# ScalarE's attention loop over 32 blocks, rolled and written out

## What is computed

```
q = apply_rope(q); k = apply_rope(k)
q = q * (1.0 / jnp.sqrt(jnp.float32(hd)))
scores = jnp.einsum('bhqd,bhkd->bhqk', q, k)
attn = jax.nn.softmax(scores, axis=-1)
out = jnp.einsum('bhqk,bhkd->bhqd', attn, v)
```

## Time and profile before

| | us |
|---|---|
| median of 3 runs (4465.53 to 4467.92) | 4466.51 |
| the profiled execution | 4463.72 |
| its span, first to last instruction | 4462.0 |
| attention's main part in it, first exponential to last copy | 685.94 to 3382.3 |
| PE busy | 4160.7 (93%) |
| DVE busy | 3137.1 (70%) |
| ACT busy | 2665.3 (60%) |

### The profile page before, as it was taken

How to read it: one execution, slowest core, us unless ns; L and a number is a source line. 1 busy time by engine, 2 the same in 40 slices (tenths; PEclk the granted TensorE clock), 3 DMA queues, 4 the chain that set the end, 5 groups by cost and what they waited for, 6 DMA issues and landing times. The chain is left out here.

```text
span 4462.0 us, 71502 instructions
## 1 busy us (share of the span) xinstructions
PE 4160.7 (93%) x23748; PEld 1788.7 (40%) x23748; DVE 3137.1 (70%) x4158; ACT 2665.3 (60%) x5113; POOL 374.6 (8%) x444
## 2 busy tenths in 40 slices
PE   6988637999999999999999999999998899999999
PEld 4666401222222222222222222222225788876666
DVE  6877596999999999999999999999950011132332
ACT  4555304778777778778778778778784222222122
POOL 0222355000000000000000000000001000011110
PEclk8999758999999999999999999999999999999999
DMA  4232393000004000004000000000004755532221
GB/s 149 76 104 90 113 152 116 6 4 4 6 4 73 12 4 4 6 4 72 14 4 4 6 4 4 6 4 4 6 4 161 230 193 195 198 100 73 64 60 40
DMA packets 206165, 264.69 MB, mean 59 GB/s; under 512 B 24880, under 2 KB 169520, under 8 KB 204240
## 3 DMA queue, kind: packets, MB, share of 16 engines
q1 hardware_dynamic: 193872, 228.98, 17.8%
q0 software_dynamic: 11904, 31.10, 2.4%
HBM read 184.76 MB, written 74.97 MB: 58 GB/s over the span
## 5 line engine op out<-in xcount | busy, mean ns | idle before, releaser
L1172 ACT ACTIVATE a_PT<-a_PS 128x512 f32<-128x512 f32 x4096 | 2119.2, 603 | 687.6 <-PE a_PS L1046 608.3
L1253 DVE TENSOR_REDUCE a_MX<-a_PS 128x2 f32<-128x1024 f32 x1062 | 1290.6, 1221 | 149.0 <-PE a_PS L1031 136.0
L1259 DVE TENSOR_REDUCE a_MX<-a_PS 128x1 f32<-128x512 f32 x1972 | 1266.7, 684 | 66.2 <-PE a_PS L1031 45.6
L1046 PE MATMUL a_PS<-a_QS,a_KS 128*128 128x512 bf16 x4096 | 1075.5, 383 | 24.2 <-ACT a_PT L1172 9.5
L1056 PE MATMUL a_OT<-a_PT,a_VG 128*32 128x512 f32 x8192 | 1095.2, 607 | 0.9 <-ACT a_PT L1172 0.8
L1031 PE MATMUL a_PS<-a_KS,a_QS 64*128 64x512 bf16 x4096 | 731.5, 393 | 111.5 <-ACT a_PT L1172 48.2
L1031 PEld LDWEIGHTS a_PS<-a_KS,a_QS 64*128 64x128 bf16 x4096 | 172.5, 93 | 1179.6 <-ACT a_PT L1172 639.7
L1046 PEld LDWEIGHTS a_PS<-a_QS,a_KS 128*128 128x128 bf16 x4096 | 314.1, 97 | 624.6 <-DVE a_MX L1253 281.3
L1444 ACT ACTIVATE e_hT<-e_up,e_BF 128x256 f32<-128x256 f32 x312 | 148.2, 475 | 413.3 <-PE e_up L1397 413.2
L1397 PE MATMUL e_up<-e_xT,e_WF 128*128 128x256 f32 x1248 | 324.7, 383 | 0.8 <-DVE e_xT L1454 0.8
L1406 PE MATMUL e_dn<-e_WP,e_hT 128*128 128x256 f32 x1248 | 322.0, 381 | 0.0
(11 more groups left out here) (222 smaller groups left out, 2783.4 us busy)
## 6 DMA issues: line engine op xcount, KB each, us to landing
e_WF<-Wfc SPq DMA_DIRECT2D x39, 1024.0 KB, 5.0
e_WP<-Wproj SPq DMA_DIRECT2D x39, 1024.0 KB, 7.0
a_QS<-scr_qparts SPq DMA_DIRECT2D x384, 32.0 KB, 9.5
a_KS<-scr_kparts SPq DMA_DIRECT2D x48, 256.0 KB, 13.3
scr_xs<-f_zero SPq DMA_DIRECT2D x1, 9984.0 KB, 33.2
e_XS<-scr_xs SPq DMA_DIRECT2D x39, 256.0 KB, 2.7
scr_ys<-e_Y SPq DMA_DIRECT2D x39, 256.0 KB, 2.1
f_X<-x SPq DMA_DIRECT2D x16, 512.0 KB, 4.7
```

The costliest lines, as they stand in the source:

```text
L1046: T.matmul(score_bank(c), KS[j][:, h, u * P:(u + 1) * P], QS[j][:, bass.ds((b * HG + h) * BLK, BLK)], start=True, stop=True).then_inc(S["q ...
L1172: nc.scalar.activation(PT[:, c % RING, :], score_bank(c), ACT.Exp, scale=SOFT_SCALE).then_inc(S["exp_done"], 1)
L1253: V.tensor_reduce(MX[n % 2][:, :, x], PS[:, banks[0]:banks[0] + SIDES, :], AX.X, ALU.max).then_inc(S["mp_free"], SIDES)
L1259: V.reduce_max(MX[n % 2][:, side, x:x + 1], PS[:, banks[side], :], AX.X).then_inc(S["mp_free"], 1)
```

## The change

The loop of ScalarE over blocks 0 to 30 becomes a Python loop, so the same instructions are written into its list 31 times. No work is added or removed on data, and the waits are the same with constants in place of registers.

```diff
@@ -1184,7 +1184,7 @@
 
             for c in range(HG):
                 exp(0, c)
-            with act.Fori(0, NG * NB - 1) as n:
+            for n in range(NG * NB - 1):
                 one_block(n, True)
             one_block(NG * NB - 1, False)
```

## The result

The changed kernel takes 4411.3 us (median of 4, 4407.56 to 4415.02), beside 4466.0 us before: ratio 0.9878, 95% interval [0.9861, 0.9895]. The profiled execution took 4407.56 us, its span is 4405.8. A second comparison gave 4410.1 against 4462.7 us, ratio 0.9888 [0.9872, 0.9905]. The forecast was 4422.5 us in a range of 4406 to 4431, so the time lies in the range and is 11 us shorter than the forecast.

What follows compares the result with a forecast made beforehand. TensorE was taken to set the pace, losing time at ScalarE's 30 branches back. From the runs' median, 4466.5 − 44 = 4422.5 us, all other terms zero; range 4406 to 4431 us.

Steps and rivals of the forecast that it cites:

- The stall is the loop's end: ScalarE's idle time between a block's final copy and chunk 4's exponential is the branch back, 1.89 us each, 30 times.
- Its size on the path: TensorE's rhythm over joints of two blocks lengthens by 1.46 us; 30 joints make 44 us.
- a loss equal to the idle time less 0.43 us: At each joint 0.43 us is slack before TensorE needs chunk 4; 1.89 − 0.43 = 1.46 us is lost.
- Nothing is late next, nothing is given back: At the joint TensorE runs on without waiting, no other engine becomes the bound; zero given back, copies 82.2 us apart.
- Registers cost nothing: Register operations beside the loop's exponentials are hidden, so replacing them by constants gains zero.
- The longer list costs nothing: ScalarE's written-out code crosses pages going straight on at zero cost; q14 moves some 90 fewer packets.
- Block 0 and the rest: Attention's first block, beside GpSimd's scatter: taken as zero change, some microseconds each way; up to 20 us possible.
- the gap isn't the loop's: Rival: the idle time between copy and exponential belongs to the hand-over and stays; 4463 to 4466 us, chance 4%.
- a branch costs a tenth of a microsecond: Other wording of a rival: branches at the joints are nearly free, so the gap stays; 4463 to 4466 us, chance 4%.
- crossings stall: Rival: ScalarE fetches each page of the straight list only on reaching it, 62 crossings add 91 us; 4513 us, chance 3%.
- part of the gain comes back: Rival: bad page crossings or a larger block 0 disturbance shrink the gain to 11 to 35 us; 4431 to 4455, chance 5%.

Runs made afterwards that it cites:

- pair: Against the kernel before, ScalarE's loop holds two blocks in a pass, 14 branches back in place of 30; 4436.4 us beside 4460.6, ratio 0.9946.
- rotate: Against the kernel before, each loop pass begins at chunk 12 in place of chunk 4, still 30 branches back; 4430.1 us beside 4462.7, ratio 0.9926.
- inner: Against the written-out list, each block gets four passes of a short loop over 24 exponentials; 4412.8 us beside 4460.6 before the change, ratio 0.9887.
- half: Against the written-out list, each block gets two passes of a loop over 48 exponentials; 4406.1 us (one run) beside 4462.7 before the change.
- hold: Loop beginning at chunk 12, plus a wait for ScalarE's own last exponential ahead of the branch; 4470.4 us (one run), kernel before the change 4440.3.

## Why the prediction was right

- **The stall is the loop's end**, with no wait behind it. Right, and shown by pair: with the same registers and the same copy, a joint without a branch has no idle time.
- **Its size on the path**, 1.46 us by 30, 44 us. The ruler gives 43.9. The step that carried it, a loss equal to the idle time less 0.43 us, holds at the joint. As a rule it isn't general: the idle time is no constant, and rotate showed 0.97 us where the rule assumed 1.9.
- **Nothing is late next, nothing is given back.** Right: the steps are 82.15 to 82.17 us, and 82.2 was forecast.
- **Registers cost nothing.** Right: the looped bodies of inner and half take as long as written-out code to 0.1 us over 30 blocks.
- **The longer list costs nothing.** Right: q14 moved 90 packets fewer, the number forecast, and no idle time of ScalarE in the 30 steps is longer than a wait for scores.
- **Block 0 and the rest**, taken as zero with some microseconds each way. This is where the time left the forecast: 4411 in place of 4422.5. In the first pair of profiles, 7.5 of the 56.2 us lie ahead of any changed instruction, and the second pair doesn't repeat them; block 0 was 2.6 and 6.4 us shorter in the two pairs, and without the scatter 0.4. The term was mis-sized: between executions and comparisons this stretch differs by more than the few microseconds allowed. The joints' 43.9 us are shown; the 9 to 11 us by which both comparisons of the change exceed them are not explained. That the time still lies in the range is in part luck: its lower end was built from ScalarE's whole idle time, 56.8 us, of which only 43.9 were on the path.
- **The rivals.** That the gap isn't the loop's, or that a branch costs a tenth of a microsecond, fell with pair; the figure of the Trainium skill, Advanced Engine Details and Errata, section Control Flow Timing, about 108 ns for a compare-and-branch, is of the right order only where the branch falls through (0.08 us to the next instruction's start) or its target is held (0.15 to 0.36 us to the body's first instruction in inner and half). A far one takes 2.4 us or more. That crossings stall fell with the ruler. That part of the gain comes back fell too. The fetch after a far branch agrees with the Trainium skill, Runtime: NRT & Kernel Launch, section Instruction fetch mechanics, which says that a target outside the pages held must be fetched first; it gives no price. The runs put 2.4 to 2.8 us from the branch to the body on it, of which the engine stood idle 0.9 to 3.0, and 4.7 to 9.6 us of idle engine beside a heavy load.

## What to carry to other kernels

A hardware loop whose body is long costs the engine a fetch at each branch back; read it as an idle time that comes once a pass where the branch stands, whatever releaser the profile names, and multiply it by the passes only after taking off the slack that the waiting engine has there. If a loop must stay, keep its body short enough to be held, or put the branch where the engine still has issued work in front of it when the sequencer gets there, behind a run of instructions whose waits are long met and not right behind a wait that ends late, and away from moments at which the DMA queues are full. A joint of the same kind without the branch (here the last, written-out block) is the cheapest witness before anything is run.

## What the runs showed of the hardware

- A branch back over 128 exponentials made ScalarE stand 1.80 to 2.08 us, over 256 of them 1.91 to 2.19 us; over 24 and 48, and onto the next instructions, nothing that can be measured.
- From a far branch to the first instruction of the loop's body it was 2.4 to 2.8 us in all kernels, when no load ran beside it, over 128 exponentials as over 256.
- The sequencer runs ahead of its engine (in rotate by 1.6 us at the branch) and stops at a wait that isn't met: the same branch left 0.97, 1.05, 1.9 or 2.76 us of idle time, by what stood ahead of it.
- While the packets of a load took 99% of the DMA engines' time, the idle time at a branch rose from 0.97 to 4.80 us, and beside the same load in hold from 2.76 to 9.60. That the fetch waits behind these packets is the likely reason; no run took the load away alone.
- The kernel before took 4466, 4461, 4463 and 4440 us in four comparisons, and its attention between the first and the 31st copy 2506.95 and 2506.70 us. Differences of 1% between kernels are better read from such a ruler than from one pair of totals.
